# Both query halves of a key block's weighted values in one slot of TensorE's loop

## The reference, cut to what matters

```python
xn = _group_norm(xf, gn_w, gn_b)
qkv = jnp.einsum('oc,bcl->bol', w_qkv, xn) + b_qkv[None, :, None]
q, k, v = (qkv[:, :ch], qkv[:, ch:2 * ch], qkv[:, 2 * ch:])
weight = jnp.einsum('bct,bcs->bts', q * scale, k * scale)
weight = jax.nn.softmax(weight.astype(jnp.float32), axis=1).astype(weight.dtype)
a = jnp.einsum('bts,bcs->bct', weight, v)
h = jnp.einsum('oc,bcl->bol', w_proj, a) + b_proj[None, :, None]
```

## Time and profile before

| | |
|---|---|
| median of 3 runs | 1505.45 us (1498.57 to 1505.92) |
| profiled execution, span | 1499.8 us |
| matmuls of TensorE | 1299.6 us, 87% of the span |
| VectorE, ScalarE, GpSimd | 71%, 60%, 24% |
| first image (50 to 189 us) | 139 us |
| middle images | 172 to 178 us each |
| last image, then epilogue | 166 us, 96 us |

### The profile page before, as it was taken

The page is one execution under the profiler, slowest core; times in us unless marked ns, Lnnn a source line. Parts: engine busy times, 40 slices in busy tenths (PEclk is TensorE's granted clock), DMA queues, the critical chain, the costliest instruction groups (busy, mean ns, idle before and its releaser), DMA issues.

```text
span 1499.8 us, 24256 instructions
## 1 busy us (share of the span) xinstructions
PE 1299.6 (87%) x8184; PEld 661.6 (44%) x8184; DVE 1059.3 (71%) x1638; ACT 894.3 (60%) x1480; POOL 359.1 (24%) x536
## 2 busy tenths in 40 slices
PE   2677898998988989899988999889898999898776
PEld 1422344544445444454435454454444644353353
DVE  1466678855897469785698668985698858885582
ACT  1356667564765657666576647657476566756422
POOL 1001004520145103340034301451033500442111
PEclk9798999999999999999999999999999999999998
DMA  5332332123220232302331233302323024110100
GB/s 188 92 84 58 81 99 74 30 57 106 64 78 8 56 114 60 82 22 63 99 99 29 57 101 69 78 8 56 114 56 86 18 65 127 45 30 0 56 2 29
DMA packets 44705, 99.01 MB, mean 66 GB/s; under 512 B 12928, under 2 KB 13184, under 8 KB 44352
## 3 DMA queue, kind: packets, MB, share of 16 engines
q1 hardware_dynamic: 41920, 87.86, 22.8%
q0 software_dynamic: 2688, 9.70, 2.2%
HBM read 22.01 MB, written 8.39 MB: 20 GB/s over the span
## 4 chain that ended last, share of the span: by engine, by line
PE 58%; DVE 17%; issue 10%; ACT 8%; SPq 3%; DMA 2%; POOL 1%; DVEq 0%; ACTq 0%; POOLq 0%
PE ps_s L551 14%; PE ps_o L566 11%; PE work L578 7%; DVE negmax L918 7%; ACT probs L790 6%; PE work L639 4%; PE work L625 3%; PE work L701 3%; PE work L706 3%; SPq L441 3%; PE work L590 3%; PE work L686 2%; PE work L613 1%; DVE ln_st L975 1%; DVE t L1057 1%
## 5 line engine op out<-in xcount | busy, mean ns | idle before, releaser
L918 DVE TENSOR_REDUCE negmax<-ps_s 128x1 f32<-128x1024 f32 x512 | 621.1, 1217 | 318.2 <-PE ps_s L551 315.2
L790 ACT ACTIVATE probs<-ps_s,negmax 128x1024 f32<-128x1024 f32 x512 | 570.1, 1114 | 397.0 <-DVE negmax L918 337.4
L551 PE MATMUL ps_s<-q_st,k_st 128*128 128x512 f32 x1024 | 402.6, 478 | 86.3 <-ACT probs L790 61.4
L551 PEld LDWEIGHTS ps_s<-q_st,k_st 128*128 128x128 f32 x1024 | 165.7, 195 | 383.3 <-ACT probs L790 217.2
L566 PE MATMUL ps_o<-probs,v_scaled 128*32 128x512 f32 x2048 | 278.7, 617 | 2.7 <-POOL v_scaled L1184 2.7
L1184 POOL TENSOR_TENSOR v_scaled<-v_tok,rsums 128x128 f32<-128x128 f32 x128 | 58.1, 454 | 718.5 <-DVE rsums L924 647.0
L578 PE MATMUL work<-xg,w_qkv 128*128 128x512 f32 x256 | 125.5, 621 | 8.2 <-ACT xg L803 6.4
L639 PE MATMUL work<-ln_ch,w_qk 128*128 128x512 f32 x232 | 113.6, 612 | 10.7 <-DVE shared L1082 7.9
L790 ACT ACTIVATION_READ_ACCUMULATOR probs<-ps_s,negmax 128x1 f32 x512 | 99.6, 194 | 0.0
L566 PEld LDWEIGHTS ps_o<-probs,v_scaled 128*32 128x32 f32 x2048 | 41.0, 109 | 110.6 <-issue 105.1
L578 PEld LDWEIGHTS work<-xg,w_qkv 128*128 128x128 f32 x256 | 50.4, 200 | 56.0 <-issue 41.1
(11 more groups left out here) (152 smaller groups left out, 1561.6 us busy)
## 6 DMA issues: line engine op xcount, KB each, us to landing
q_st<-hi SPq DMA_DIRECT2D x124, 128.0 KB, 2.4
q_st<-lo SPq DMA_DIRECT2D x124, 128.0 KB, 2.4
k_st<-hi SPq DMA_DIRECT2D x240, 64.0 KB, 2.0
k_st<-lo SPq DMA_DIRECT2D x240, 64.0 KB, 2.0
xg<-in_x POOLq DMA_DIRECT2D x8, 1024.0 KB, 6.8
x<-in_x SPq DMA_DIRECT2D x8, 1024.0 KB, 5.2
out_x<-x SPq DMA_DIRECT2D x16, 512.0 KB, 3.5
con<-in_consts SPq DMA_DIRECT2D x1, 1826.0 KB, 11.1
```

Source lines behind the costliest of these rows:

```text
L551: mm = pe.matmul(ps_s[s % 2][:, half * HALF:half * HALF + HALF], k_st[:, h, j * P:j * P + P], q_st[g][:, h, half * HALF:half * HALF + HALF ...
L790: act.activation(probs[:, j % 2, h, :], ps_s[s % 2][:, :], ACT.Exp, bias=negmax[:, s % 4:s % 4 + 1], accum_out=sums[:, j % 2, h:h + 1]).th ...
L918: dve.tensor_reduce(negmax[:, s % 4:s % 4 + 1], ps_s[s % 2][:, :], AX_X, ALU.max, negate=True)\
```

## The change

`weigh_values` loses its argument `half` and does both halves, one after the other, in slot 2 of the next block; slot 3 has none. The wait for the scaled values stands once ahead of both, the wait for the copy of a half stands ahead of that half. The epilogue's call is the same work as before. Nothing else of the kernel is changed, and the counts of `pv_done` stay two a block.

```diff
-            def weigh_values(i, g, j, half):
+            def weigh_values(i, g, j):
 
                 n = 2 * NB * i + NB * g + j
-                if half == 0:
-                    pe.wait_ge(v_scaled_ready, n + 1)
-                if j == 0 and not (isinstance(i, int) and i == 0 and g == 0):
-
-                    pe.wait_ge(att_done, 4 * i + 2 * g - 1 + half)
-                cols = slice(half * HALF, half * HALF + HALF)
-                for h in range(HG):
-                    mm = pe.matmul(ps_o[D * h:D * h + D, cols], v_scaled[:, j % 2, D * h:D * h + D],
-                                   probs[:, j % 2, h, cols], start=(j == 0), stop=(j == NB - 1))
-                mm.then_inc(pv_done, 1)
+                pe.wait_ge(v_scaled_ready, n + 1)
+                for half in range(2):
+                    if j == 0 and not (isinstance(i, int) and i == 0 and g == 0):
+
+                        pe.wait_ge(att_done, 4 * i + 2 * g - 1 + half)
+                    cols = slice(half * HALF, half * HALF + HALF)
+                    for h in range(HG):
+                        mm = pe.matmul(ps_o[D * h:D * h + D, cols], v_scaled[:, j % 2, D * h:D * h + D],
+                                       probs[:, j % 2, h, cols], start=(j == 0), stop=(j == NB - 1))
+                    mm.then_inc(pv_done, 1)
...
-                    if s % HG >= 2:
+                    if s % HG == 2:
                         n = s // HG - 1
                         if n >= 0:
-                            weigh_values(i, n // NB, n % NB, s % HG - 2)
+                            weigh_values(i, n // NB, n % NB)
                         elif kind != "first":
-                            weigh_values(i - 1, NG - 1, NB - 1, s % HG - 2)
+                            weigh_values(i - 1, NG - 1, NB - 1)
...
-                for half in range(2):
-                    weigh_values(B - 1, NG - 1, NB - 1, half)
+                weigh_values(B - 1, NG - 1, NB - 1)
```

## The result

The changed kernel is slower: 1559.07 us, median of 4 runs (1550.59 to 1568.74), against 1505.68 us of the kernel before (4 runs, 1498.57 to 1510.17). The ratio is 1.0368, with a 95% interval of 1.0323 to 1.0414. The forecast was 1510, the range 1491 to 1525. The profiled execution has a span of 1551.7 us, 51.9 more than before. One of e8's four runs (1533.46 us) was in a slower state than the others and is left out everywhere.

A forecast was written before the change was run, and what follows sets the result against it. Bounds: TensorE's dense middle iterations and the score-to-exp round trip. First iteration +5 us and the others near zero gave 1504.8 from a 1499.8 us span; the runs' median lies 5.65 above that span, so 1510, range 1491 to 1525.

The forecast's parts named there:

- Step (2): Score(4q) comes 0.86 us later behind half b: +5 us in the first image, +3.1 us in a middle one.
- step (5): Middle images: TensorE's saving of 0.23 us a block counts where TensorE sets the end, -2.2 us an image.
- Step (1): TensorE, slots 2 and 3 without tiles: 3.32 us becomes 3.09 with joined halves, -0.23 us a block.
- Step (3): Slots 35 and 27 of middle images: moving half b ahead fills TensorE's waits there, -0.7 us an image.
- Step (4): ScalarE's exp held by half b, 56.9 us of waits: relief taken as -0.5 us an image.
- The rival: First image: three thin slots in a row lower TensorE's clock, +11 us each tenth; chance 0.31 with late scores.
- The scores come too late: Score(4q) late and 4q+1 right behind it move the wait to TensorE: +19 us, 1524; chance 0.31 with the clock.
- TensorE's saving wins: Fewer drains between kinds of matmul on TensorE outweigh the first image's loss: -12 us, 1493; chance 0.28.
- Pairs 1.86 us apart: Sign in TensorE's profile after: joined halves start 1.86 us before the next score.
- Score(37) 1 us earlier: Sign at the filled group-mean wait of slot 35: score(37) about 1 us earlier after score(35).
- First image 3 to 8 us longer: Sign of the later score(4q) in the first image: its length grows by 3 to 8 us.
- Middle ones within 1.5: Sign for the middle images: length within 1.5 us of 174; over 2 longer means the delay went down the chain.

The follow-up runs named there:

- e8: Kernel before with both halves joined in slot 2 of the first image only; 1518.14 us, ratio 1.0134 (3 runs).
- e1: Kernel before with half b moved ahead of slot 3's tiles, still behind score(4q), half a unmoved; 1530.30 us, ratio 1.0138.
- e4: Kernel before with both halves joined in slot 2 only within slots 32 to 63 of every image; 1521.94 us, ratio 1.0094.
- e9: Kernel before with useless matmuls fitted to its idle time in slots 25, 33 and 41; 1505.64 us, ratio 0.9995.
- e6: Kernel before with two useless 448-column matmuls in each wait of slots 25, 33 and 41; 1504.03 us, ratio 1.0003.
- e11: e9 with one more useless 448-column matmul in each of 14 slots of the first image; 1499.43 us, ratio 0.9958 to the kernel before.
- e3: Kernel before with both halves joined in slot 2 only within slots 0 to 31 of every image; 1521.81 us, ratio 1.0101.

## Why the prediction was wrong

Two steps of the sum failed and one term was missing. Step (2) put the middle images' losses where nothing lasting was lost, and had no term for the tiles that half b passes; step (5) counted a saving that went into waits; and a lower clock in the middle and last images was put at nothing, where the runs show it as the largest part.

**Step (1), TensorE's own time: right.** TensorE of after in time, middle image, slots 10 to 13:

```profile
588.49 1.92 PE L566 MATMUL ps_o<-probs,v_scaled 128*32 128x512 f32 x16
590.35 1.20 PE L551 MATMUL ps_s<-q_st,k_st 128*128 128x512 f32 x4
591.38 1.88 PE L625 MATMUL work<-att,w_proj 128*128 128x512 f32 x4
...
593.92 0.63 PE L613 MATMUL work<-con,tok 128*128 128x128 f32 x4 [0.67 <-DVE tok L985]
```

The joined halves take 1.86 us until the scores (588.49 to 590.35), as in the earlier trace rows. The two scores behind them stand back to back, 0.56 apart (590.35 and 590.91 in the single records, which this row takes together). So 0.23 us a block are saved, 29 us over 127 blocks.

**Step (2), scores(4q) later: right for the first image, at the wrong places in the middle ones.** The first image is 9.8 us longer, of it 7.0 us x 0.38 = 2.7 by the clock, so 7 by the order; the sum said +5, with bounds 0 and 12. In a middle image the sum had +3.1, at units 8 and 12 and at 16, 56 and 60. Those up to unit 16 came in part and did not last: score(17) is 1.0 us late where +1.4 was expected, and nothing of it is left at unit 24. At units 56 and 60 nothing came. These are stretches of middle images that lie wholly at the full clock (units 0 to 4 are left out, as the wait between two images varies there), from the start of one unit's L918 reduction to another's (L917 in after), in us:

| units | before | after | e1 |
|---|---|---|---|
| 4 to 24 | 46.8 | 46.8 | 46.5 |
| 24 to 33 | 24.8 | 25.3 to 25.9 | 25.9 to 26.1 |
| 33 to 45 | 32.15 | 32.7 | none at full clock |
| 45 to 52 | 19.3 | 20.1 | 19.3 |
| 52 to 63 | 36.7 | 36.8 | 36.8 |

The walk looked only at what the later *score* does. Half b also went ahead of the *tiles* of slot 3, in slots 31 and 39 too, and those feed tiles two slots later. TensorE of after at slot 41 of image 3:

```profile
672.72 0.49 PE L686 MATMUL work<-kv_c,shared 128*128 128x128 f32 x2 [1.61 <-DVE den L1039]
```

What lasts is lost between units 24 and 52, +1.9 to +2.5 us an image, for which the sum had nothing but (3)'s gain. From 24 to 33 it is the tiles: e1, which moves b past them alone, loses at least as much there. From 45 to 52 it isn't: e1 loses nothing and e4, which has the halves joined there, loses the same 0.8, so it comes with both halves ahead of the scores. From 33 to 45 e4 shows after's 32.7; no run parts that stretch between tiles and scores.

The later scores opened waits too, which the walk had not followed through VectorE. VectorE and TensorE of after in slot 8 of image 3:

```profile
581.41 1.23 DVE L917 TENSOR_REDUCE negmax<-ps_s 128x1 f32<-128x1024 f32 x1 [2.33 <-PE ps_s L551]
...
582.64 0.72 DVE L954 SCALAR_TENSOR_TENSOR lo<-work,par,hi 128x512 fp32r<-128x512 f32 x1
...
583.41 0.66 PE L605 MATMUL work<-con,x 128*128 128x128 f32 x4 [1.14 <-DVE lo L954]
```

And the same tile in e1, where it doesn't wait:

```profile
570.41 0.66 PE L605 MATMUL work<-con,x 128*128 128x128 f32 x4
```

Score(8) came late, so VectorE's reduction of it came late, and behind that the step (L954) that frees the tile's bank. These 1.14 us are among those given back by unit 24: a new wait is a loss only if it is still there some units on.

**Step (3), filled waits: right in place.** Slot 35's wait went from 1.30 us to 0.44 and score(37) came 1.1 us earlier against its neighbours, as stated; slot 27's wait of 0.33 is gone. Against these, waits in slots 8, 33, 41 and 50 grew by 0.8 to 1.1 us each.

**Step (4), exp held by half b: right in kind.** That wait has gone (56.9 us to 1.7), and TensorE's for exponentials rose by 27.9 us (10 or more expected).

**Step (5), the saving on the path: failed.** 0.23 x 16 x 0.59 counted a saving where the chain ran over TensorE before. After the change TensorE waits more in every middle image, 17.8 to 22.4 us of idle between matmuls against 13.8 to 17.2. The 2.2 us went into those waits. The middle images' order sum is +1.9 at the slope of 0.44 where 0 stood (six times: +11), the last one's about +2. With the first one's 7, the images give 20 us of order, and the runs 20.6.

**The term that was missing: the clock.** The rival was named, but for the first image alone, whose clock went from 0.87 to 0.86 only. It was priced for no other image, since at 91% busy I held the middle ones to be safe. There the low level rose from 34 us in six images to 82 (sums of the table's rows), and from 3.4 to 20.5 in the last. Over the whole runs it is 86.4 us more; at 0.38 us per us the clock is the largest part, 33 of 53.5 us, of which the fills took back 23. The rival's mechanism, three thin slots in a row, isn't needed for it: e1 lost clock with the halves spread, 37.8 us at the low level. Whether it adds to the 86.4 of the change no run shows apart from the waits. By the Trainium skill, page TensorE: Matmul & The Clock Gate, Terms, the penalty is about the throttled time times one minus the ratio, which is 0.5 here; the runs show 0.38; presumably part of the slower matmuls lies beside waits, which no run tested.

**The rivals.** "The scores come too late", 1524, had the sign and, with +19, nearly the order's part (+20.6). In the middle images that is luck: its 3.1 us stood at places that lost nothing lasting. "TensorE's saving wins" is out: it needs middle images shorter than 174, none is. The order sum missed by some 15 us, the clock by 33.

**Against the signs set beforehand.** Pairs 1.86 us apart: yes. Score(37) 1 us earlier, ScalarE's waits gone, TensorE's waits for exp up by 10 or more: yes. First image 3 to 8 us longer: 9.8, 7 without the clock. Middle ones within 1.5: no, 180.3 against 174.9 in the mean. By the prediction's own words the delay then went down the chain and (5) was no gain; that is so for some 2 us of the 5.4, the rest is the clock.

**What stays open:** why the clock falls lower in some images than in others with the same code (images 1, 5 and 6 of after), why e8's runs with its code differ by 19 us, and why e9's first image, whose code is that of before, has 14.6 us less at the low level and is 4 us shorter. For the last, one profile of each kernel can't tell a cause from the spread between runs.

## What to carry to other kernels

When a step is moved ahead in an in-order queue, list every instruction that it passes and price the consumers of each, not only those of the one that it was put in front of: here the tiles that were passed opened the waits of slots 33 and 41, and the passed scores, through VectorE, that of slot 8. Then compare stretches at one clock level, and follow a loss until it is given back or not. On a TensorE that is 85 to 91% busy and still at full clock, put a price on added idle time beyond the idle time itself, by measuring how much of the existing runs' spread goes with the granted clock. A wait that can't be removed can be filled with matmuls that compute nothing: it took back 23 of 53 us here, and in the kernel before, with its shorter waits, the same fills gave nothing (e6, e9); only those in its first image gave 6 (e11).

## What the runs showed of the hardware

- Behind 10 us with TensorE's matmuls 90% busy (8.98 of 10.00), a wait of 1.67 us was followed by some 10 us at the low level (clock 0.56 from 283 to 294 us). I had expected this only of thin stretches like the first image.
- Most of the spread between runs of one and the same kernel goes with the time at the low level: spans of 1494.5 to 1513.2 us with clocks of 0.973 to 0.962 (25 runs, correlation 0.92).
- The losses at the low level do not add: +10.5 us for joining the first 32 units, +23.2 for the second 32, +86.4 for both (e3 and e4 against the runs on their own chip: +3.7 and +16.4).
- Two halves of 32-column matmuls joined take 1.86 us, apart 2.00, and the scores ahead of them are 0.09 us shorter without a half behind.
